# Linear attention: the 64 repeated columns written by one ScalarE copy instead of four activations

## The reference

```python
h = h + _L0_ffn_ref(_layernorm(h, axis=-1), ...)            # experts, ends in its own layer norm
h = h + _L1_attn_ref(_layernorm(h, axis=-1), L1_attn_w_qkv, L1_attn_w_proj, L1_attn_b_proj)

def _L1_attn_ref(x, w_qkv, w_proj, b_proj):                 # 12 heads of 16 columns
    qkv = x @ w_qkv.T
    q = _l1_normalize(q); k = _l1_normalize(k)              # each column divided by its sum of |.| over the tokens
    kv = jnp.einsum('bhnd,bhne->bhde', k, v)
    out = jnp.einsum('bhnd,bhde->bhne', q, kv)
    return out.reshape(B, N, C) @ w_proj.T + b_proj
```

## Time and profile before

| what | value |
|---|---|
| median of three executions | 2638.91 us |
| the profiled execution | 2633.06 us |
| its span, first to last instruction | 2631.2 us |
| TensorE busy | 2242.1 us (85%) |
| VectorE busy | 1924.3 us (73%) |
| ScalarE busy | 1593.7 us (61%) |
| GpSimd busy | 1017.1 us (39%) |
| mean granted TensorE clock | 0.909 of full speed |
| second linear attention, xn of the first chunk to xn of the last | 1831.87 to 2156.35 us |

### The profile page before, as it was taken

The page is one execution under the profiler, slowest core; times in us unless marked ns, Lnnn a source line. Parts: engine busy times, 40 slices in busy tenths (PEclk is TensorE's granted clock), DMA queues, the critical chain, the costliest instruction groups (busy, mean ns, idle before and its releaser), DMA issues. The chain is left out here.

```text
span 2631.2 us, 45404 instructions
## 1 busy us (share of the span) xinstructions
PE 2242.1 (85%) x14046; PEld 1623.8 (62%) x14047; DVE 1924.3 (73%) x5417; ACT 1593.7 (61%) x2815; POOL 1017.1 (39%) x1100
## 2 busy tenths in 40 slices
PE   8999999999998799999982999991788887766665
PEld 4444444444443688888871899991677784544443
DVE  5777777777774588898882666663668878888886
ACT  2444444444444588888871677773778865667776
POOL 1100100100000156666664577776545542344333
PEclk9999999999999899999995999995779998877766
DMA  2000000000000423323334788878566620000000
GB/s 59 1 19 13 0 19 13 1 9 1 1 0 1 111 52 74 77 67 76 75 71 137 233 261 260 257 240 138 78 79 91 90 27 11 22 22 22 27 22 27
DMA packets 114524, 183.10 MB, mean 70 GB/s; under 512 B 14338, under 2 KB 84327, under 8 KB 114079
## 3 DMA queue, kind: packets, MB, share of 16 engines
q0 software_dynamic: 74816, 86.34, 17.5%
q1 hardware_dynamic: 39556, 94.85, 11.4%
HBM read 64.46 MB, written 64.39 MB: 49 GB/s over the span
## 5 line engine op out<-in xcount | busy, mean ns | idle before, releaser
L213 ACT ACTIVATE prob<-pscore 128x896 f32<-128x896 f32 x336 | 308.2, 917 | 423.5 <-PE pscore L295 423.5
L420 DVE TENSOR_REDUCE pmax<-ppre 112x1 f32<-112x512 f32 x656 | 424.5, 686 | 162.1 <-PE ppre L262 162.0
L309 PE MATMUL pout<-prob,xkey 128*64 128x448 f32 x1344 | 328.0, 567 | 0.4 <-ACT prob L213 0.4
L262 PE MATMUL ppre<-xh,yh 49*112 49x512 f32 x656 | 291.1, 446 | 7.8 <-DVE pmax L420 4.2
L1578 POOL DMA_INDIRECT rows_out<-yb,home3b x252 | 247.4, 982 | 115.6 <-issue 60.1
L195 POOL CAST yh<-ynext 113x448 fp32r<-113x448 f32 x28 | 17.2, 614 | 667.5 <-DVE pmax L420 639.4
L737 POOL DMA_INDIRECT rows_in<-xr,idx x224 | 215.8, 964 | 118.1 <-DVE idx L1269 54.1
L262 PEld LDWEIGHTS ppre<-xh,yh 49*112 49x112 f32 x656 | 112.6, 172 | 239.4 <-issue 103.5
L295 PE MATMUL pscore<-yh,xh 49*128 49x448 f32 x700 | 241.0, 422 | 0.4 <-DVE yh L440 0.4
L1885 POOL TENSOR_TENSOR sums<-rows,gout 112x512 f32<-112x512 f32 x112 | 141.0, 1269 | 257.1 <-DVE rows L2513 257.1
L295 PE MATMUL pscore<-yh,xl 49*128 49x448 f32 x700 | 202.4, 364 | 0.0
(11 more groups left out here) (394 smaller groups left out, 6583.9 us busy)
## 6 DMA issues: line engine op xcount, KB each, us to landing
wd<-down SPq DMA_DIRECT2D x63, 512.0 KB, 3.0
xb<-rows_in SPq DMA_DIRECT2D x63, 455.0 KB
sums<-rows_out POOLq DMA_DIRECT2D x56, 336.0 KB, 6.2
h<-brow POOLq DMA_DIRECT2D x28, 336.0 KB, 5.3
h<-gambet POOLq DMA_DIRECT2D x28, 336.0 KB, 4.9
out<-sums SPq DMA_DIRECT2D x28, 336.0 KB, 2.8
rows_in<-zero SPq DMA_DIRECT2D x15, 455.0 KB, 6.2
rows_out<-yb,home3b POOLq DMA_INDIRECT x252
```

Of the source, the lines that this page charges most:

```text
L213: nc.scalar.activation(prob[j % 3][:, :, :], pscore[j % 2][:, :, 0:CH], ACT.Exp).then_inc(exped, 1)
L262: pe.matmul(out[:, :], yh1[rows, q * T:(q + 1) * T], xh[b % 2][rows, block * 512:(block + 1) * 512], start=True, stop=True, tile_position= ...
L309: mm = pe.matmul(pout[i * LO:(i + 1) * LO, 0:CH], xkey[b % 2][:, 2 * j + i, :], prob[j % 3][:, i, :], start=(j == 0), stop=(i == 1 and j = ...
L420: nc.vector.reduce_max(pmax[:, q, 2 * block + half:2 * block + half + 1], bank(u, depth), AX.X).then_inc(pre_max, 1)
```

## The change

The four activations that write the columns 192 to 255 of xn (from the columns 128 to 191 of h, with the same scale and offset as before) are taken out. In their place one ScalarE copy takes the columns 128 to 191 of xn, for all four tiles at once, to the columns 192 to 255. The copy reads what the four remaining activations have just written, so the last of these adds to a new semaphore, `xn_rows`, and ScalarE waits for it before the copy. The semaphore for the readers, `xn_ready`, is added to by the copy.

```diff
-                 "off4_out", "xn_ready", "xtr_mm", ...
+                 "off4_out", "xn_rows", "xn_ready", "xtr_mm", ...
...
-                for cols, src in ((slice(0, D), slice(0, D)), (slice(D, 256), slice(128, D))):
-                    for q in range(TPC):
-                        t = g * TPC + q
-                        ac = nc.scalar.activation(xn[g % 2][:, q, cols], h[:, t, src], ACT.Identity,
-                                                  bias=off4[:, q:q + 1], scale=rst4[:, q:q + 1])
-                ac.then_inc(S["xn_ready"], 1)
+                for q in range(TPC):
+                    t = g * TPC + q
+                    ac = nc.scalar.activation(xn[g % 2][:, q, 0:D], h[:, t, :], ACT.Identity,
+                                              bias=off4[:, q:q + 1], scale=rst4[:, q:q + 1])
+                ac.then_inc(S["xn_rows"], 1)
+                act.wait_ge(S["xn_rows"], g + 1)
+                nc.scalar.copy(xn[g % 2][:, :, D:256], xn[g % 2][:, :, 128:D]).then_inc(S["xn_ready"], 1)
```

More of the change, by code:

```diff
@@ L1766, in attention_and_ffn_phase @@
                  "rst_out", "off_out", "nrm_out", "dvec3", "hm_out", "stat4_out", "agg4_out", "veps4_out", "rst4_out",
-                 "off4_out", "xn_ready", "xtr_mm", "xH_out", "xL_out", "xT_out", "qk_mm", "b_sum", "a_sum",
+                 "off4_out", "xn_rows", "xn_ready", "xtr_mm", "xH_out", "xL_out", "xT_out", "qk_mm", "b_sum", "a_sum",
                  "g_mm", "g_out", "gt_mm", "gt_out", "t2_mm", "t2_out", "kv_mm", "kv_out", "m1_mm", "m1_out",
```

## The result

| | before | after |
|---|---|---|
| median of 7 executions each | 2637.86 us | 2602.91 us |
| all 7 | 2627.19 to 2641.04 | 2599.89 to 2617.76 |
| ratio after to before, 95% interval | | 0.9898, [0.9867, 0.9928] |
| profiled execution | 2633.06 us | 2601.11 us |
| its span | 2631.2 us | 2599.3 us |

Faster, by 1.0% of the time: 26.9 us by the ratio, which is one of means (19 to 35 us by its interval), 35 us by the medians, 31.9 us by the two spans. Of the spans' difference 26.5 us lie in the stretch that the prediction was about; of the other 5.4, 0.9 is the step of the last chunk behind the stretch, and 4.5 lie in stages that do the same work as before.

What follows compares the result with a forecast made beforehand. The prediction took ScalarE's ring with VectorE to bound the kernel: 25 chunks times 0.85 us, less 0.3, is 20.9 us, taking the mean of 2634.5 to 2613.6, said as 2614 us; range of 8 in 10, 2603 to 2624.

Steps and rivals of the forecast that it cites:

- the stretch: From the xn of chunk 1 to the xn of chunk 26 in the linear attention, where the saving was expected.
- What bounds the step: Linear attention: ScalarE's ring with VectorE sets the 10.91 us step; time taken from ScalarE there shortens it by as much.
- The saving of a chunk: Writing xn on ScalarE: 3.08 us becomes 2.23, so 0.85 us less per chunk, bounds 0.80 to 0.87.
- The dearer wait: Copy would start 0.05 to 0.10 us after the activations, so 25 chunks save 0.5 to 1.8 us less; not adopted.
- The cut in two steps: Two steps where the next image begins: TensorE's 0.69 us wait limits the saving, 0.3 us lost in all.
- If TensorE's clock stays as it is: Condition on the saving of 19.7 to 21.5 us: TensorE's clock does not change.
- the sum of 20.9 us: Whole saving: 25 chunks on the chain times 0.85 us, less 0.3 us for two steps.
- the early steps win more: Rival, chance 0.08: four early steps reach TensorE's high clock, winning 6.1 us more, 2606 us.
- TensorE fills the late steps: Rival, chance 0.09: from step 9 on TensorE has no slack, only 8 early chunks save, 6.8 us, giving 2626 us.
- The clock falls in the late steps: Rival, chance 0.04: late steps drop to TensorE's low clock, each losing 2.07 us; with all 16, 2659 us.
- The median: Whole kernel: forecast 2614 us, from the four executions' mean of 2634.5 less 20.9; chance 0.78.
- Nothing moves outside the stretch by more than the spread of the runs: Other stages, including the feed-forward stage, should keep their times within the runs' spread, 12 us; otherwise the sum is wrong.

Runs made afterwards that it cites:

- the clock held in the early steps: Kernels before and after, each with eight unread matmuls added on TensorE in steps 1 to 7: medians 2633.81 and 2599.36 us, stretch 296.6 and 274.9 us.
- the wait alone: Kernel before, all eight activations kept, with only ScalarE's wait for its own semaphore put between the first four and last four: 2640.89 us, one run.

## Why the prediction came out as it did

- *What bounds the step* was right, and it is shown now, not only read: the step grows by what ScalarE is held longer (0.14 and 0.31 us), shrinks by what it is held less (0.88, 1.02, 1.32), and does not care that xn comes later.
- *The saving of a chunk*, 0.85 us, measured 0.88 to 0.89, just above its upper bound of 0.87. The wait was priced right: its copy starts 0.03 us after the activations, and alone it costs 0.14, not 0.12. The 0.04 came from the copy's end: 0.31 us to the next instruction's start, where line 985 had 0.35.
- *The dearer wait*, which "Advanced Engine Details and Errata", section "Network/Comms", in the Trainium skill would have made of 50 to 100 ns for reading a semaphore, did not show: 0.03 us of idle time before each copy. The estimate by that page, 19.2 to 20.4 us, would have been further off.
- *The cut in two steps* (0.3 us) was wrong. TensorE's wait of 0.69 us counts from the modelled end of the matmul ahead, and one that follows without a wait starts before that end: 2006.12 to 2005.92 + 0.37 is 0.17 us of overlap. The real slack was 0.86 us, and the step gave its whole 0.88.
- *"If TensorE's clock stays as it is"* was the step of the sum that failed. It did not stay: the sum of 20.9 us met 26.5 in the stretch, of which 22.0 are the sum's own term at its measured size and 4.5 the clock. The rival "the early steps win more" was not another case but a part of what happened: 2.8 of its 6.1 us came in the early steps, and 1.7 more in three late steps, which no rival had. With the clock held in the early steps, the two kernels differ by 21.7. "TensorE: Matmul & The Clock Gate", section "Part 1: The HAM clock gate", in the Trainium skill says that activity lifts the clock, and the traces agree: 0.78 to 0.81 by the change, 0.78 to 0.95 by the added matmuls.
- *TensorE fills the late steps* did not come, though it now ends the chain in two of them. *The clock falls in the late steps* did not come: 1.00 there after the change, where the kernel before had three late steps at about 0.85.
- *The median*, 2602.91 us, is 11 us below the 2614 that was forecast and 0.1 below the lower end of its range, 2603. The forecast was reckoned from a mean, 2634.5, and the seven executions before have that mean again. The seven after have 2607.5, which is 27.0 us less and 6.1 below the 2613.6 of the sum; 5.6 of the 6.1 are the stretch (26.5 for 20.9, from one profile each). That the median lies another 4.6 us below the mean is the draw of seven executions: four lie at 2599.89 to 2602.91, three at 2612.09 to 2617.76.
- *Nothing moves outside the stretch by more than the spread of the runs*: so it was, but the spread there is wide. In the profiles of all the kernels here, from the xn of chunk 26 to the end takes 478 to 491 us, for nearly the same work. It goes with TensorE's clock: from its first rounding to the end, the feed-forward stage takes 427.6 us at a granted clock of 0.76 and 433.7 at 0.72, the shortest and the longest of all (the changed kernel with matmuls ahead of it, and the wait alone):

```profile
2171.01:2598.60 427.59, 274.28 (x1641) 194.00 (x1640) 362.57 (x950) 299.23 (x517) 171.50 (x137) 0.76 0.08 23
```
```profile
2205.34:2639.05 433.71, 283.47 (x1641) 197.67 (x1640) 361.52 (x950) 299.34 (x517) 171.64 (x137) 0.72 0.08 23
```

In the three pairs of profiles (plain, with early matmuls, with matmuls ahead of the feed-forward stage) the kernel before took 5.4, 7.2 and 7.6 us more outside the stretch, of which 0.9 is the last chunk's step. Whether the rest is chance or comes of the change was not settled.

## What to carry to other kernels

Where one engine goes round a ring with one short wait in it, count how long each instruction holds that engine, start to next start, and expect the step to change by just that, also for an instruction whose result nobody is waiting for. A copy of finished columns in the place of activations that compute them again pays, and the wait that it needs on its own engine costs 0.14 us here, which goes away when other work stands between (or with the copy on an engine with time to spare, even if it is twice as slow there). Where the chain runs through matmuls at TensorE's low clock, give the clock a term of the sum with both signs: taking work from another engine can raise it, and it was about a sixth of the gain in the stretch here.

## What was not expected of the hardware

Matmuls that nobody reads made a kernel faster: 56 of them in the kernel before gave 8.2 us in the stretch, and 0.9967 [0.9945, 0.9989] in the time.

The same way between two stages ran at either level of the clock. Two stretches of the kernel before with the added early matmuls, on the way to the feed-forward stage, and the same two of the kernel before with matmuls on that very way:

```profile
2157.00:2173.00 16.00, 13.91 (x71) 10.61 (x71) 11.65 (x36) 4.02 (x10) 2.90 (x1) 0.85 0.01 1
2173.00:2193.00 20.00, 20.00 (x56) 13.80 (x56) 9.86 (x29) 3.28 (x7) 2.92 (x3) 0.50 0.00 0
```
```profile
2158.00:2174.00 16.00, 16.00 (x102) 15.41 (x101) 11.22 (x30) 8.63 (x21) 10.55 (x1) 1.00 0.00 1
2174.00:2194.00 20.00, 18.55 (x104) 13.25 (x102) 16.55 (x55) 5.12 (x12) 2.54 (x3) 1.00 0.00 1
```

In the first, TensorE was granted 0.50 (1.2 GHz) for the whole 20 us, with 100% busy time for 56 matmuls; in the second 1.00, for 104. In the first the way from the xn of chunk 26 to the feed-forward stage takes 60.3 us, in the second 51.2. In this case's profiles it took 49.8 to 51.3 us eleven times and 54.2, 59.4 and 60.3 once each. The last three come from kernels without added matmuls there, whose work on that way is that of eight of the eleven. The three profiles with them were all short; that is too few to call it their doing.
